# A fused token mixing, gated linear attention and mixture-of-experts block on one Trainium2 core: the five hand-kept instruction orders of the attention part laid out anew

## The reference

```python
h = einsum('bhid,oi,od->bho', x, weighted_sum, weight)     # tokens; one matmul over 1024 inputs
h = concatenate([h, txt], axis=1)                          # 4 x 544 x 256
y = layernorm(h)
q, k, v, g = y @ Wq, y @ Wk, y @ Wv, y @ Wg                # 16 heads of 16
gk = log_sigmoid(y @ Wg1 @ Wg2 + bg2) / 16
S = exp(gk_t) * S + k_t v_t^T ;  o_t = S q_t * 0.25        # scan over the 544 rows of an image
o = o * rsqrt(mean(o*o) + eps) * g_norm_w                  # per head
h = h + (o * silu(g)) @ Wo
y = layernorm(h)
top 2 of 8 experts by y @ Wr, each expert takes at most 680 rows, softmax weights
h = h + sum of weight * ((silu(y_e @ W1) * (y_e @ W3)) @ W2)
```

## Time and profile before

| | us |
|---|---|
| median of 3 runs | 689.18 (687.34 to 699.11) |
| profiled execution, its own time | 687.07 |
| its span | 685.3 |
| attention part, up to the first expert matmul | 334.92 |
| expert part | 350.38 |
| PE busy, share of the span | 602.3, 88% |
| DVE, ACT, POOL busy | 374.7, 330.4, 347.7 |
| mean granted PE clock | 0.946 of full speed |

### The profile page before, as it was taken

One profiled execution on the slowest core, in us unless ns is written; L12 is line 12 of the kernel. 1 busy time (PEld: TensorE's weight loads), 2 busy tenths in 40 slices (PEclk: granted clock), 3 DMA queues, 4 the chain that ended last, 5 costly groups with the idle time before them and its releaser, 6 DMA issues.

```text
span 685.3 us, 14471 instructions
## 1 busy us (share of the span) xinstructions
PE 602.3 (88%) x5058; PEld 560.2 (82%) x5058; DVE 374.7 (55%) x943; ACT 330.4 (48%) x870; POOL 347.7 (51%) x416
## 2 busy tenths in 40 slices
PE   4999999999879957840699999999999999999991
PEld 3998789689867845520599999999999999999991
DVE  4666665767846754871264563745637355473530
ACT  4496476638557721210263563626536264462520
POOL 5003311320366854014295785977859688596321
PEclk9999999999999977965699999999999999999997
DMA  8511030212201100101516235263342625322011
GB/s 271 199 63 65 21 111 2 64 50 82 64 2 33 36 2 2 39 28 48 173 60 181 55 120 97 59 181 62 127 82 60 188 54 168 41 95 32 8 17 24
DMA packets 49157, 52.49 MB, mean 77 GB/s; under 512 B 16576, under 2 KB 37616, under 8 KB 49104
## 3 DMA queue, kind: packets, MB, share of 16 engines
q1 hardware_dynamic: 39312, 40.94, 18.9%
q0 software_dynamic: 8704, 9.81, 8.2%
q10 hardware_dynamic: 1088, 1.05, 0.5%
...
## 4 chain that ended last, share of the span: by engine, by line
PE 73%; issue 10%; POOL 6%; DVE 4%; DMA 3%; ACT 3%; SPq 0%; POOLq 0%; DVEq 0%; ACTq 0%
PE ps L1628 42%; PE ps L1670 17%; POOL slot_table L932 3%; PE ps L1794 2%; PE ps L1835 2%; POOL sb_rounded L870 2%; PE ps L1740 2%; PE ps L1849 2%; PE ps L1830 1%; PE ps L1646 1%; DMA sb_tokw<-in_L_tok_weight 1%; DMA sb_att<-xn_rows,sb_g_index 1%; PE ps L1810 1%; PE ps L1842 1%; PE ps L1757 1%
## 5 line engine op out<-in xcount | busy, mean ns | idle before, releaser
L1628 PE MATMUL ps<-sb_xe_hi,sb_rounded 128*128 128x340 f32 (+1 forms) x1024 | 216.4, 303 | 0.3 <-issue 0.2
L1628 PEld LDWEIGHTS ps<-sb_xe_hi,sb_rounded 128*128 128x128 f32 x1024 | 169.7, 189 | 2.0 <-issue 1.1
L1628 PE MATMUL ps<-sb_xe_lo,sb_rounded 128*128 128x340 f32 (+1 forms) x512 | 153.9, 301 | 0.0
L1670 PE MATMUL ps<-sb_rounded,sb_h_hi 128*128 128x256 f32 (+1 forms) x640 | 117.4, 285 | 0.0
L1228 DVE TENSOR_TENSOR sb_dec<-ps,sb_gate 128x340 f32<-128x340 f32 (+1 forms) x128 | 60.0, 469 | 81.7 <-ACT sb_gate L992 78.8
L1628 PEld LDWEIGHTS ps<-sb_xe_lo,sb_rounded 128*128 128x128 f32 x512 | 96.8, 189 | 0.0
L1670 PEld LDWEIGHTS ps<-sb_rounded,sb_h_hi 128*128 128x128 f32 (+1 forms) x640 | 95.5, 181 | 0.0
L992 ACT ACTIVATE sb_gate<-ps 128x340 f32<-128x340 f32 (+1 forms) x128 | 53.2, 415 | 80.5 <-PE ps L1628 77.1
L1670 PE MATMUL ps<-sb_rounded,sb_h_lo 128*128 128x256 f32 (+1 forms) x320 | 89.8, 281 | 0.0
L1235 DVE TENSOR_TENSOR sb_h_lo<-sb_dec,sb_h_hi 128x340 fp32r<-128x340 f32 (+1 forms) x128 | 89.2, 696 | 0.2
L858 POOL DMA_INDIRECT out_rows<-sb_att,sb_s_index x40 | 62.8, 1570 | 51.7 <-DVE sb_att L1243 46.2
...
## 6 DMA issues: line engine op xcount, KB each, us to landing
...
```

The source lines that it names most:

```text
L1628: ins = pe.matmul(out_ap, lhs, rhs, start=(i == 0), stop=(i == n - 1))
L1670: ins = pe.matmul(ps[BANK[s]][0:r, 0:D], hh[:, f, o:o + r], w2s[:, f, ww, :], start=(f == 0 and i == 0), stop=(f == FT - 1 and i == 2))
```

## The change

All five orders are written anew, with other banks behind the @ signs. Beside them:

- The loads of the projection weights move from ACT's queue to SP's, as the step `w5_load`; `decay_load` and `tok_load` now stand before the second x tile and before them.
- `ACT_BANKS = (1, 0, 0, 2)`: of the four banks of `scores`, ACT and POOL take one for image 0, none for images 1 and 2, two for image 3 (before: one for images 0 to 2, none for image 3). DVE takes the rest, and tile 4's four small instructions become one.
- For image 3 `state` goes by ACT and POOL where DVE did it alone. `og` moves from POOL to DVE for images 1 and 2. `ln2_apply` runs on ACT for images 0 and 3 (before POOL and DVE).
- `LN2_BATCH` is cut differently: image 0 in three batches, image 2 as (0, 1, 2) and (3, 4), image 3 with tile 0 alone.
- PE waits for banks 0 to 3 before it reads the flag of `exact` rather than inside the block that is jumped over.

```diff
@@ the orders, cut to the places spoken of
-PE_ORDER: x_turn.0.1.0@4 x_turn.0.0.0@5 ... g1_turn@0 we_turn.0@1 ... embed.0.1@3
+PE_ORDER: g1_turn@4 g1_mul@5 we_turn.0@6 we_turn.1@7 we_turn.2@4 we_turn.3@5 x_turn.0.0.0@6 ... embed.0.0@5 embed.0.1@6
-SP_ORDER: load_x.0.1 load_x.0.0 tok_load load_txt.0 decay_load last_load load_x.0.2 load_x.0.3
+SP_ORDER: load_x.0.1 decay_load tok_load load_x.0.0 w5_load last_load zero_rows.1 load_txt.0 table_load load_x.0.2 zero_rows.0 load_x.0.3
-POOL_ORDER: ... w13_split.0 w13_split.1 w13_split.2 w13_split.3 ... w13_split.7 q_mask.3.0 q_mask.3.1 table_scatter.12
+POOL_ORDER: ... table_scatter.8 state.2.3 q_mask.3.1 w13_split.0 ln2_apply.2.1 w13_split.1 ln2_apply.2.2 q_mask.3.0 ln2_apply.2.0
+            w13_split.2 w13_split.3 table_scatter.3 table_scatter.9 ln2_apply.2.4 ln2_apply.2.3 w13_split.4 state.3.0 w13_split.5
-DVE_ORDER: ... router.2.4 top2.1 weigh.1 exact.3 slots.1 scores.3.0 state.3.0
+DVE_ORDER: ... exact.3 router.2.2 router.2.0 ln2_newton.2.1 scores.3.1 scores.3.0 router.2.4 router.2.3 state.3.0 top2.1 state.3.1
...
@@ -246,14 +247,17 @@
+    if kind in ("x_turn", "we_turn") and not on("dve", *step):
+        return [("act", step)]
...
 LN1_BATCH = [(4, 0, 1), (2, 3)]
-LN2_BATCH = [[(0, 1), (2, 3, 4)], [(0, 1), (2, 3, 4)], [(0, 1), (2, 3, 4)], [(0, 1), (2, 3), (4,)]]
+LN2_BATCH = [[(0,), (1, 2), (3, 4)], [(0, 1), (2, 3, 4)], [(0, 1, 2), (3, 4)], [(0,), (1, 2), (3, 4)]]
 ROUNDS = [(0, 10), (10, 15), (15, 18), (18, 20)]
+ACT_BANKS = (1, 0, 0, 2)
...
+                elif kind == "w5_load":
+                    for n, w in enumerate((wq, wk, wg, wv)):
+                        sp.dma_start(raw13_w[n], w.rearrange("(h p) o -> p h o", p=P)).then_inc(ready["w5_in"], 16)
...
@@ pool, scores
-                    low = att[:, (NC * b + c) % 2, 3, :, :]
+                    low = att[:, (NC * b + c) % 2, 4 - ACT_BANKS[b]:4, :, :].rearrange("p j n t -> p (j n) t")
...
@@ scalar
-            for n, w in enumerate((wq, wk, wg, wv)):
-                act.dma_start(raw13_w[n], w.rearrange("(h p) o -> p h o", p=P)).then_inc(ready["w5_in"], 16)
...
+                elif kind == "ln2_apply":
+                    b, c = at
+                    r = CH[c]
+                    need("dve", "ln2_newton", b, batch_of(1, b, c))
+                    need("pe", "xn2_turn", b - 1, c)
+                    if b:
+                        act.wait_ge(xn_stored[c], 16 * b)
+                    finish(act.activation(xn2[0:r, c, :], h[b % 2][0:r, c, :], ACT.Identity,
+                                          bias=nmr[0:r, 1, b % 2, c:c + 1], scale=rstd[0:r, 1, b % 2, c:c + 1]), "act", step)
...
@@ vector, scores
-                    banks = 3 if on("act", *step) else 4
+                    banks = 4 - ACT_BANKS[b]
...
-                        for j in range(4):
-                            ins = dve.tensor_tensor(att[0:r, i, j, :, 0:r],
...
+                        ins = dve.tensor_tensor(att[0:r, i, :, :, 0:r], ps_all[0:r, 0:4, 0:4 * r].rearrange("p j (n t) -> p j n t", n=4),
...
@@ tensor
                     def exact_pe():
-                        bank_free(step, need.inside)
...
+                    bank_free(step, need)
                     exact_path(pe, need, b, exact_pe)
```

More of the change, by code:

```diff
@@ L146 @@
-ln2_stats.1.0 scores.1.4 mix.1.3 ln2_newton.1.0 attn_out.1.2 ln2_stats.1.2 mix.1.4 ln1_stats.2.2 attn_out.1.3
-ln2_stats.1.3 ln1_stats.2.3 attn_out.1.4 ln2_stats.1.4 xn_turn.2.0 xn_turn.2.4 ln2_newton.1.1 xn_turn.2.1
-ln1_newton.2.1 router.1.0 router.1.1 x_turn.3.1.0 x_turn.3.0.0 ln1_stats.3.4 xn_turn.2.3 xn_turn.2.2
-x_turn.3.0.1 x_turn.3.1.1 router.1.2 router.1.3 decay_sum.2.0 decay_sum.2.1 k_proj.2.0.0 k_proj.2.0.1 router.1.4
-top2.0 range.2 k_proj.2.1.1 weigh.0 range_sum.2 k_proj.2.1.0 q_proj.2.1.0 q_proj.2.1.1 q_proj.2.0.1 q_proj.2.0.0
@@ L156 @@
-router.2.0 ln2_newton.2.1 k_proj.3.1.0 range.3 k_proj.3.0.1 k_proj.3.1.1 range_sum.3 k_proj.3.0.0 router.2.2
-router.2.3 q_proj.3.0.1 q_proj.3.0.0 q_proj.3.1.1 q_proj.3.1.0 router.2.4 top2.1 weigh.1 exact.3 slots.1
-scores.3.0 state.3.0 scores.3.1 state.3.1 mix.3.0 og.3.0 state.3.2 mix.3.1 attn_out.3.0 ln2_stats.3.0 og.3.1
-scores.3.2 attn_out.3.1 ln2_stats.3.1 scores.3.3 ln2_newton.3.0 state.3.3 mix.3.3 ln2_apply.3.0 mix.3.2 og.3.2
-og.3.3 ln2_apply.3.1 scores.3.4 attn_out.3.2 ln2_stats.3.2 router.3.0 attn_out.3.3 ln2_stats.3.3 mix.3.4
@@ L161 @@
-ln2_newton.3.1 og.3.4 router.3.1 ln2_apply.3.2 ln2_apply.3.3 attn_out.3.4 ln2_stats.3.4 router.3.2
-ln2_newton.3.2 router.3.3 top2.2 ln2_apply.3.4 weigh.2 slots.2 router.3.4 top2.3 weigh.3 slots.3 counts
+we_prod.0 we_prod.1 g1_mul constants we_turn.0 we_turn.1 we_turn.2 we_turn.3 x_turn.0.0.0 x_turn.0.0.1
+w5_split.3 x_turn.0.1.0 x_turn.0.1.1 w5_split.2 w5_split.1 ln1_stats.0.4 ln1_stats.0.0 w5_split.4 ln1_stats.0.1
+x_turn.0.2.1 x_turn.0.2.0 ln1_stats.1.4 x_turn.0.3.1 x_turn.0.3.0 ln1_newton.0.0 ln1_stats.0.2 ln1_stats.0.3
@@ new lines @@
+x_turn.2.1.0 mix.0.1 mix.0.2 attn_out.0.0 ln2_stats.0.0 attn_out.0.2 ln2_stats.0.2 state.0.2 xn_turn.1.3
+x_turn.2.0.0 xn_turn.1.2 ln2_newton.0.0 xn_turn.1.0 x_turn.2.1.1 state.0.3 attn_out.0.1 ln2_stats.0.1
+decay_sum.1.1 ln1_stats.2.0 scores.0.3 k_proj.1.1.1 ln2_newton.0.1 scores.0.4 decay_sum.1.0 mix.0.4 mix.0.3
+q_proj.1.0.1 attn_out.0.3 ln2_stats.0.3 x_turn.2.2.0 q_proj.1.1.0 k_proj.1.0.0 k_proj.1.1.0 router.0.0 range.1
+attn_out.0.4 ln2_stats.0.4 q_proj.1.0.0 range_sum.1 ln2_newton.0.2 k_proj.1.0.1 router.0.1 q_proj.1.1.1
@@ new lines @@
+ln1_stats.3.0 xn_turn.2.3 router.1.0 x_turn.3.2.0 xn_turn.2.2 x_turn.3.2.1 x_turn.3.1.1 attn_out.1.3
+ln2_stats.1.3 router.1.1 ln2_newton.1.1 decay_sum.2.0 ln1_stats.3.4 decay_sum.2.1 k_proj.2.0.0 q_proj.2.0.1
+router.1.2 ln1_stats.3.2 q_proj.2.1.1 k_proj.2.1.0 range.2 q_proj.2.1.0 q_proj.2.0.0 range_sum.2 k_proj.2.0.1
+ln1_stats.3.1 x_turn.3.3.0 k_proj.2.1.1 x_turn.3.3.1 exact.2 ln1_newton.3.0 router.1.4 router.1.3 top2.0
+scores.2.0 ln1_stats.3.3 state.2.0 ln1_newton.3.1 scores.2.2 state.2.1 weigh.0 slots.0 mix.2.0 xn_turn.3.3
@@ new lines @@
+xn_turn.3.2 og.2.0 xn_turn.3.0 xn_turn.3.1 xn_turn.3.4 mix.2.2 og.2.2 attn_out.2.0 ln2_stats.2.0 scores.2.1
+attn_out.2.2 decay_sum.3.0 ln2_stats.2.2 state.2.2 mix.2.1 decay_sum.3.1 og.2.1 k_proj.3.0.0 k_proj.3.1.1
+attn_out.2.1 q_proj.3.1.1 ln2_stats.2.1 q_proj.3.0.1 q_proj.3.1.0 scores.2.3 state.2.3 ln2_newton.2.0
+k_proj.3.0.1 range.3 scores.2.4 mix.2.3 q_proj.3.0.0 range_sum.3 og.2.3 mix.2.4 k_proj.3.1.0 router.2.1 og.2.4
+attn_out.2.3 ln2_stats.2.3 attn_out.2.4 ln2_stats.2.4 exact.3 router.2.2 router.2.0 ln2_newton.2.1 scores.3.1
@@ L163 @@
+scores.3.0 router.2.4 router.2.3 state.3.0 top2.1 state.3.1 scores.3.2 mix.3.0 weigh.1 state.3.2 og.3.0 mix.3.1
+slots.1 og.3.1 attn_out.3.0 ln2_stats.3.0 scores.3.3 ln2_newton.3.0 state.3.3 attn_out.3.1 mix.3.2 og.3.2
+mix.3.3 scores.3.4 ln2_stats.3.1 attn_out.3.2 ln2_stats.3.2 mix.3.4 og.3.3 ln2_newton.3.1 og.3.4 attn_out.3.3
+ln2_stats.3.3 router.3.0 attn_out.3.4 ln2_stats.3.4 router.3.1 router.3.2 top2.2 ln2_newton.3.2 weigh.2 slots.2
+router.3.4 router.3.3 top2.3 weigh.3 slots.3 counts
 """
@@ L926, in _ @@
                     need("dve", "slots", rnd)
[L927 to L929 removed]
+                    need.once(ready["table_out"], 16)
+                    if rnd not in settled:
+                        settled.add(rnd)
                         settle(pool)
```

235 lines of the change are left out of this document (111 added, 124 removed).

## The result

The changed kernel takes 693.96 us (median of 4 runs, 692.81 to 696.06) where the kernel before takes 688.41 (the three runs above and one more). The ratio is 1.0078, 95% interval 1.0048 to 1.0109: a little slower, and less than 2% from no change. I had forecast 671 and a range of 660 to 686: wrong, in size and in sign. In two later sets the same pair gave 1.0027 (0.9992 to 1.0063) and 1.0035 (1.0001 to 1.0069).

A forecast was written before the change was run, and what follows sets the result against it. PE's throughput was taken to bound the middle and waits the two ends. Terms -3.0 - 1.0 - 6.4 - 1.5 - 5.5 = -17.4 gave 669.7 for the profiled execution, stated as 671 us; range 660 to 686.

The forecast's parts named there:

- Step 2: Dense middle, first token matmul to image 3's flag: idle PE time shrinks, added DVE and POOL work mostly covered; -1.0 us.
- step 4: Image 3's attention and routing behind its flag: routing fills DVE's idle time; 46.1 us in place of 51.6, -5.5.
- the 7.55 us of the earlier trace: Two waits around 260 to 269 us, PE and ACT standing too; half was counted as gain.
- Step 1: The start: token weights load earlier, first token matmul at about 14.3 instead of 16.55 us, g1_mul into the wait; -3.0.
- Step 3: PE's wait at image 3's flag: round 1's routing moves behind the flag, 8.0 us becomes 1.6; -6.4.
- the earlier flag: Two routers and two transposes move behind image 3's flag, so it is reached 1.5 us earlier; -1.5.
- My 46.1 us for the stage: Forecast length of image 3's attention and routing, from the flag to the end of slots.2, instead of 51.6 us.
- my 32.5: Forecast of DVE's busy us in image 3's stage up to slots.2, against 33.5 before.
- Step 5: Behind slots.2: ten closing scatters still follow at POOL's pace, round 1's remaining eight are covered; 0 us.
- POOL holds image 3: Rival, chance 0.20: POOL's block of 16 scatters makes image 3's masks late; six us late give 677, range 675 to 685.
- The jumps cost what they cost: Rival, chance 0.12: image 3's two waits, 7.55 us, belong to the kept jumps and stay; 675, within 673 to 678.
- DVE becomes the bound: Rival, chance 0.09: added DVE work in images 1 and 2 and image 3's routing surface; 692, up to 700.

The follow-up runs named there:

- e9: The changed kernel unaltered, as control beside the kernel before in one set: 690.50 us, ratio 1.0035 to the kernel before (687.67).
- e10: The changed kernel with the 30 table scatters of rounds 0 and 1 left out: 662.99 us, ratio 0.9657 to the kernel before.
- e11: The kernel before with the same 30 table scatters of rounds 0 and 1 left out: 673.47 us, ratio 0.9799 to the unaltered kernel before.
- e12: The changed kernel with POOL's order alone altered, scatters in pairs with other POOL work between: 668.36 us, ratio 0.9735 to the kernel before.
- e17: The kernel before with round 1's routing behind image 3's flag and the 30 scatters of rounds 0 and 1 left out: 674.54 us, ratio 0.9795.
- e7: The kernel before with the changed kernel's start alone, its lists up to image 0's tokens: 688.29 us, ratio 0.9981.
- e6: The kernel before unaltered, run for its trace: 690.54 us in the traced run.

## Why the prediction was wrong, step by step

**Where it failed.** Step 2 put POOL's block of 16 at 20.0 us of POOL's own time, covered by 220 matmuls of PE. The 20 us were right (201.30 to 222.10), and nobody waited for POOL: it came out of the block and waited 10.37 us for ACT. What had no price, in step 2 and in step 4, was what such a block does to the other engines: 27.5 us in the changed kernel (e9 less e10), where the old blocks cost 14.2 (e11). The second failure is step 4, the overlap: routing on DVE was to fill idle time behind the flag, and half of the 7.55 us of the earlier trace rows was booked as waits that a new order fills. Those waits were a crawl under the ten scatters of round 1, which began at 254.63, 8 us before, and the routing lies on the chain. Put together: the orders alone are worth 10.5 us (e10 against e11), not 17.4, and their blocks cost 13.3 us more than the old ones, which leaves 2.8 us slower, as e9 measured. Free of scatters the flag's first matmul comes 14.2 us earlier (233.78 against 247.97), where steps 1 to 3 and the earlier flag had 11.9; all that is missing is missing behind it. Without the scatters image 3's stage of the kernel before takes 43.33 us instead of 51.60; with the change and without them, 45.49; the changed kernel in pairs, 45.55. In this order, e11, e10, e12:

```profile
247.97:291.30 43.33, 33.75 (x348) 24.73 (x348) 33.60 (x111) 10.45 (x31) 0.00 (x1) 0.82 0.08 27
```

```profile
233.78:279.27 45.49, 36.12 (x364) 26.43 (x364) 34.74 (x128) 19.96 (x52) 13.93 (x18) 0.82 0.09 30
```

```profile
237.40:282.95 45.55, 34.09 (x364) 24.39 (x364) 35.47 (x128) 19.87 (x52) 25.10 (x30) 0.89 0.10 30
```

My 46.1 us for the stage are near the 45.5 of a kernel that doesn't crawl, but by luck: what had to go from the old 51.60 was a crawl, and no new order fills that. Against the old stage free of scatters the new one is 2.2 us longer, not 5.5 shorter, and its DVE load is 2 to 3 us above my 32.5. That routing moved in here goes onto the chain is shown by e17 below (49.4 us for this stage).

**Step 1 (-3.0): in part, and not where I put it.** The terms that I gave add up to 13.9 for the first token matmul, not to 14.3. It starts at 16.37:

```profile
9.52 3.64 PE L1736 MATMUL ps<-sb_ident,sb_att 128*128 128x128 f32 x16 [0.34 <-DVE sb_att L1290]
...
16.37 0.83 PE L1641 MATMUL ps<-sb_rounded 128*128 128x256 f32 x5 [0.46 <-DVE sb_rounded L1313]
```

I counted four plus two subtractions at 0.62 us. The high half on ACT (0.60) has to be finished before each low half, and they alternate at 0.86 us apiece. What was won is the order behind: 48 token matmuls in a row, image 0's tokens done at 30.90 instead of 32.78 (1.9 us), and by e7 against e6 at 30.5 instead of 33.6. On the whole kernel e7 gives 1.3 us, and its interval leaves 3 open.

**Step 2 (-1.0).** In e10 PE idles for 7.0 of the 217.8 us from its first token matmul to the flag, in e11 for 7.5 of 222.3 up to where it stands. The kernel before had 11.1, so some 4 of those were a crawl too, and of the DVE load added in images 1 and 2 nothing shows. In the changed kernel the stretch is 15.5 us longer than in e10: PE idles for 14.8 us (233.30 - 218.55) instead of 7.0, and is busy for 218.55 instead of 210.8, at a granted clock of 0.96 instead of 1.00.

**Step 3 (-6.4): right, and given back.** No wait for `sb_cum` is left ahead of the flag; PE's last wait there is 0.86 us. In e17 alone the flag's first matmul comes at 241.36 instead of 248.02, and the first closing scatter at 290.76 instead of 291.30: of 6.7 us, 6.1 are returned. DVE and PE of e17:

```profile
246.96 0.19 DVE L1558 TENSOR_REDUCE sb_tops<-sb_lg 128x5 f32<-128x40 f32 x1
...
251.07 2.28 DVE L1477 TENSOR_TENSOR sb_att<-ps,sb_upper 128x2048 f32<-128x2048 f32 x1
```

```profile
253.41 1.22 PE L1843 MATMUL ps<-sb_sq,sb_blocks 128*128 128x256 f32 x2 [3.81 <-DVE sb_att L1477]
```

4.1 us of routing stand ahead of a tile's mask, and PE waits 3.81 us for the mask. Whether the smaller masks and states of step 4 make the move pay, no run takes apart.

**Step 5 (0): right.** The ten closing scatters run at 1.25 us from 308.93, started by `sb_slot_of`, with nothing left to crawl; this stage and its gathers take 30.84 us, 30.31 before.

**The rivals.** "POOL holds image 3" (0.20) had the right block and the wrong mechanism: PE and ACT never waited for POOL, DVE for 0.6 us. "The jumps cost what they cost" (0.12) is refuted: e10 keeps the jumps over all four flags' blocks, and PE waits on "issue" for 2.9 us in all. The rule that I set beside it, of the Trainium skill (Runtime: NRT & Kernel Launch, Instruction fetch mechanics), is that a jump out of the fetched code stalls the engine. In e10 no more than 1.2 us of idle time on "issue" stands before the first matmul behind a jump, and the 7.55 us of the kernel before went with the scatters (e11). "DVE becomes the bound" (0.09): between 120 and 140 us, in image 1's attention, DVE is busy for 14.56 of 20 us (14.57 before), and PE for all 20. None of my cases held the mechanism that took the gain away.
